# Attention scores as fp16 products over 96 stacked rows per head, in place of fp32 products with block-diagonal keys

## The chip, the cores and the metric

The kernel runs on one NeuronCore of one Trainium2 chip. The metric is the device time of one execution in microseconds (us). TensorE is called PE in the profile, its weight loads PEld, VectorE is DVE, ScalarE is ACT, GpSimd is POOL, and SyncE, which only issues DMA transfers here, is SP. A letter q behind an engine (SPq) marks its instruction queue.

## What is computed

One transformer layer on 4096 tokens of width 512: cross-attention with 16 heads of 32 over a context of 128 positions per batch, and then a feed-forward part with a router, the two best of eight experts, and a shared expert. The change touches only the attention scores.

```python
def _L0_xattn_ref(query, key, value, pad_mask, subsq_mask, Wq, bq, Wk, bk, Wv, bv):
    q = (query @ Wq.T + bq).reshape(n, s, H, d).transpose(0, 2, 1, 3)
    k = (key @ Wk.T + bk).reshape(n, t, H, d).transpose(0, 2, 1, 3)
    v = (value @ Wv.T + bv).reshape(n, t, H, d).transpose(0, 2, 1, 3)
    att = jnp.einsum('bhsd,bhtd->bhst', q, k) / jnp.sqrt(jnp.float32(d))
    att = jnp.where(pad_mask == 0, jnp.float32(-1000000000.0), att)
    att = jnp.where(subsq_mask == 0, jnp.float32(-1000000000.0), att)
    prob = jax.nn.softmax(att, axis=-1)
    out = jnp.einsum('bhst,bhtd->bhsd', prob, v)
...
x = x + jnp.tanh(g_xattn[0]) * _L0_xattn_ref(_layernorm(x, axis=-1), ctx_1024, ctx_1024, ...)
x = x + jnp.tanh(g_ffn[0]) * _L0_ffn_ref(_layernorm(x, axis=-1), ...)
```

## The kernel before

The work is written out by hand for each engine, with semaphores between them. Every engine has one block of code, and inside it the order of the instructions is the order of the source.

Pass 1 handles 32 tiles of 128 tokens: layer norm, queries, attention, second layer norm, router. It is a software pipeline over iterations `it`. In one iteration an engine works on several tiles at once, each at another stage, and a stage with lag L handles tile `it` - L. The helper `pipeline` (L289) writes iterations 0 to 11 out, runs 12 to 31 as a loop of ten pairs (v=0 and v=1), and writes the tail out. Passes 2 (experts, 71 slots) and 3 (shared expert, 32 tiles) follow; they start only when all engines have finished pass 1.

The stages of pass 1 that matter here, by lag:

- Lag 0: SP loads the tile (L377), DVE computes its statistics (L865, L873).
- Lag 2: PE transposes the normed tile into bank 0 (L1038). ACT takes its fp16 high half `x_hi` (L554), DVE the low half `x_lo` (L806). PE computes the queries, transposed, into bank 0 with 48 fp16 matmuls (L1121 to L1123). At the end of its iteration ACT copies them with scale and bias into the fp32 tile `q_t` (four instructions, L605) and raises `q_ready`.
- Lag 3: PE computes the scores of four head groups (`scores(k)`, L1090). Each is one fp32 product of 128 rows and 512 columns: the queries of four heads against `kbd`, which holds the keys of the four heads on the diagonal of 32-row blocks and zeros elsewhere. DVE adds the mask and takes each head's maximum (`maxima(k)`, L776, sixteen instructions a tile). POOL subtracts the maxima (L467), ACT takes exponents (L568, L598).
- Lags 4 to 8: probabilities are transposed and multiplied with the values (L1108), normalised (L788, L790), added to x (L826), normed (L802), routed (L862 and after). SP stores results (L367, L371, L373).

What sets the order around the change: on PE the new tile's transposes (which wait for `q_ready` of the tile before, because bank 0 must be free), two probability transposes, `scores(0)`, `scores(1)`, `mix_values(0)`, `scores(2)`, and so on. DVE's body begins with L802, L806 and `maxima(0)` and ends with `normalise(0, 4)` (L788, L790). Extra work hangs behind the body: the maxima of raw weights in iterations 2 to 10 (L879, 2.27 us each) and a weight split in each second iteration of the loop (L907, 2.35 us). Ahead of tile 0 the keys are computed by PE (L1064), and DVE writes them into `kbd` with sixteen instructions (L757).

## Time and profile before

| what | us |
|---|---|
| median of 3 runs | 1160.58 (1155.75 to 1164.13) |
| the profiled execution, its own time | 1157.58 |
| its span, first to last instruction | 1155.8 |
| pass 1, from the first to the last `maxima` | 44.6 to 491.9 |

The span is the stretch that the trace covers; the execution's own time is 1.8 us more. The times of this document are counted from the span's start. A row's mean duration is that of one instruction and includes the time in the pipeline, so the pace of a row of matmuls is read from their starts. The granted clock is 1.00 when TensorE runs at 2.4 GHz and 0.50 at 1.2 GHz.

### The profile page before, as it was taken

Reading aid. Unit: us, or ns where it says so; the run is one execution under the profiler, and the core shown is the slowest. Engines: PE = TensorE matmul, PEld = TensorE weight load, DVE = VectorE, ACT = ScalarE, POOL = GpSimd, SP = SyncE. Lnnn points to the kernel's source line nnn. Section 1 sums busy time; section 2 is a strip of 40 time slices with the busy share of each in tenths; the row PEclk is TensorE's granted clock in tenths of the full one; section 3 lists DMA queues with packets and bytes.
Section 4 is the critical chain, followed back from the end, with each engine's and each line's share of the span. In section 5 each row is a group of like instructions: output and inputs, shape, how many; then the busy total and the mean of one; then the engine's idle time right before and its main releaser. Section 6 shows DMA issues by size and latency. Waiting matters only on the chain.

```text
span 1155.8 us, 26617 instructions
## 1 busy us (share of the span) xinstructions
PE 1050.2 (91%) x7344; PEld 677.3 (59%) x7345; DVE 822.7 (71%) x2938; ACT 531.4 (46%) x1041; POOL 441.8 (38%) x654
## 2 busy tenths in 40 slices
PE   4699979999999999860899999999999999999997
PEld 3488767777777777660455555555554444444443
DVE  5899868788888888763576666666665666666666
ACT  1366546666666666640444444444443232232322
POOL 3254647676667667442112112112110423232322
PEclk9999889999999999855899999999999999999999
DMA  7555573223323223432233333333332544444543
GB/s 290 197 177 179 131 173 95 93 93 93 93 93 94 94 93 110 101 102 72 74 110 118 115 113 118 118 109 118 118 109 67 185 158 161 157 168 149 169 149 128
DMA packets 76731, 146.96 MB, mean 127 GB/s; under 512 B 20912, under 2 KB 23088, under 8 KB 73872
## 3 DMA queue, kind: packets, MB, share of 16 engines
q1 hardware_dynamic: 46512, 66.01, 20.0%
q10 hardware_dynamic: 17280, 44.83, 10.5%
q0 software_dynamic: 12896, 35.58, 9.9%
q8 instruction: 22, 0.36, 0.2%
q14 instruction: 21, 0.17, 0.1%
HBM read 94.04 MB, written 52.35 MB: 127 GB/s over the span
## 4 chain that ended last, share of the span: by engine, by line
PE 64%; issue 11%; DVE 9%; POOL 8%; ACT 4%; DMA 2%; POOLq 1%; another core or an unknown queue 1%; SPq 0%; DVEq 0%; ACTq 0%
PE bank L1046 15%; PE bank L1047 15%; PE bank L1048 15%; PE bank L1038 8%; PE bank L1090 3%; PE bank L1108 3%; DVE arena L776 3%; POOL arena L467 3%; POOL token_of_row L503 2%; ACT arena L605 1%; DVE arena L865 1%; POOL arena L474 1%; DMA token_of_row<-arena 1%; DVE peak L879 1%; PE bank L1064 1%
## 5 line engine op out<-in xcount | busy, mean ns | idle before, releaser
L1046 PE MATMUL bank<-weights,arena 128*128 (+1 forms) x682 | 259.9, 381 | 2.1 <-ACT arena L647 1.9
L1047 PE MATMUL bank<-weights,arena 128*128 (+1 forms) x682 | 259.8, 381 | 0.0
L1048 PE MATMUL bank<-weights,arena 128*128 (+1 forms) x682 | 259.6, 381 | 0.0
L1038 PE MATMUL bank<-ident,arena 128*128 128x128 f32 (+1 forms) x1592 | 189.4, 267 | 56.1 <-DMA arena<-normed_rows,arena 25.7
L1038 PEld LDWEIGHTS bank<-ident,arena 128*128 128x128 f32 (+1 forms) x1592 | 161.4, 132 | 103.0 <-issue 71.9
L514 POOL DMA_INDIRECT arena<-normed_rows,arena x71 | 67.1, 946 | 254.9 <-PE bank L1038 238.7
L1108 PEld LDWEIGHTS bank<-arena 128*128 128x128 f32 x1024 | 131.7, 198 | 34.3 <-issue 29.5
L1090 PE MATMUL bank<-arena 128*128 128x512 f32 x256 | 138.8, 647 | 5.4 <-DVE arena L776 5.1
L1108 PE MATMUL bank<-arena 128*128 128x33 f32 x1024 | 128.8, 276 | 2.9 <-issue 1.8
L467 POOL TENSOR_TENSOR arena<-arena 128x512 f32<-128x512 f32 x96 | 101.3, 1056 | 76.8 <-DVE arena L776 75.7
L524 POOL DMA_INDIRECT arena<-expert_rows,arena x64 | 62.8, 981 | 173.9 <-DVE arena L998 156.1
L776 DVE CUSTOM_DVE_ANT_0 arena<-bank,arena 128x128 f32<-128x128 f32 x512 | 116.8, 283 | 15.2 <-PE bank L1090 11.1
L568 ACT ACTIVATE arena<-arena 128x512 f32<-128x512 f32 x96 | 60.6, 631 | 119.0 <-POOL arena L467 118.7
L1048 PEld LDWEIGHTS bank<-weights,arena 128*128 128x128 f16 x682 | 67.0, 98 | 80.9 <-issue 1.5
L1046 PEld LDWEIGHTS bank<-weights,arena 128*128 128x128 f16 x682 | 67.1, 98 | 72.1 <-issue 4.4
L1047 PEld LDWEIGHTS bank<-weights,arena 128*128 128x128 f16 x682 | 67.0, 98 | 69.8 <-issue 1.3
L970 DVE TENSOR_SCALAR arena<-bank,arena,w_back 128x512 f32<-128x512 f32 x71 | 57.5, 810 | 55.6 <-PE bank L1048 55.5
L1121 PE MATMUL bank<-arena 128*128 128x128 f16 x512 | 89.2, 221 | 1.4 <-DVE arena L806 1.4
L1122 PE MATMUL bank<-arena 128*128 128x128 f16 x512 | 89.2, 221 | 0.0
L1123 PE MATMUL bank<-arena 128*128 128x128 f16 x512 | 89.1, 221 | 0.0
L503 POOL DMA_INDIRECT token_of_row<-arena x64 | 66.4, 1038 | 39.8 <-POOL arena L500 17.9
L656 ACT ACTIVATE arena<-arena 128x256 f16<-128x256 f32 x71 | 36.0, 508 | 91.3 <-DVE arena L982 91.3
(175 smaller groups left out, 1895.7 us busy)
## 6 DMA issues: line engine op xcount, KB each, us to landing
expert_rows<-arena ACTq DMA_DIRECT2D x71, 256.0 KB, 2.1
arena<-in_x SPq DMA_DIRECT2D x64, 256.0 KB, 3.2
weights<-in_w_gu ACTq DMA_DIRECT2D x8, 1024.0 KB, 4.7
x_rows<-arena SPq DMA_DIRECT2D x32, 256.0 KB
normed_rows<-arena SPq DMA_DIRECT2D x32, 256.0 KB, 4.9
normed_transposed<-arena SPq DMA_DIRECT2D x32, 256.0 KB, 2.3
arena<-normed_transposed SPq DMA_DIRECT2D x32, 256.0 KB, 3.3
arena<-x_rows SPq DMA_DIRECT2D x32, 256.0 KB, 3.4
```

The costliest lines, as they stand in the source:

```text
L467: g.tensor_tensor(sc, sc, mx, ALU.subtract).then_inc(shift_done, 1)
L503: g.indirect_dma_start(list_dram, bass.IndirectOffsetOnAxis(ap=row_i[u][:, k:k + 1], axis=0), tok_i[u], None).then_inc(rows_out[u], 16)
L776: last = d.tensor_tensor_reduce(score[u][:, hh * T:(hh + 1) * T], bank[2 + k % 2][:, h * T:(h + 1) * T], mask_bias[u], 1.0, LOWEST, ALU.ad ...
L1038: last = t.transpose(dst[:, c * P:(c + 1) * P], src[:, c * P:(c + 1) * P], (ident16 if src.dtype == F16 else ident)[:, :])
L1046: t.matmul(dst, hi[:, rows], w_hi(c), start=(c == 0), stop=False)
L1047: t.matmul(dst, hi[:, rows], w_lo(c), start=False, stop=False)
L1048: last = t.matmul(dst, lo[:, rows], w_hi(c), start=False, stop=(c == chunks - 1))
L1090: t.matmul(bank[2 + k % 2][:, :], q_t[u][:, k * P:(k + 1) * P], kbd[:, u, k, :], start=True, stop=True).then_inc(s_done, 1)
L1108: last = t.matmul(bank[6 + half][:, at:at + D + 1], probs_t[k % 2][:, h * P:(h + 1) * P], vaug[:, u, k * HG + h, :], start=True, stop=True)
L1121: t.matmul(dst, wq[:, 0, at:at + P], x_hi[:, xs], start=(ci == 0), stop=False)
L1122: t.matmul(dst, wq[:, 0, at:at + P], x_lo[:, xs], start=False, stop=False)
L1123: last = t.matmul(dst, wq[:, 1, at:at + P], x_hi[:, xs], start=False, stop=(ci == EC - 1))
```

## The change

The scores are computed in fp16 halves. The queries are split: ACT writes the high half of bank 0 into `q_halves` with one instruction, DVE subtracts it and writes the low half, as the last instruction of its body. The product high*high + low*high + high*low is one product over 96 rows when the halves stand under each other: queries as (high, low, high), keys as (high, high, low). For this the rows of four heads, which stand in four blocks of 32 partitions, must be moved into the same 96 partitions. SP does it with twelve DMA transfers for each tile, each of 32 partitions (`stack`). PE then computes each head's scores with one fp16 matmul of 96 rows and 128 columns, sixteen a tile. The bias of the queries goes into the product as a fifth kind of matmul (64 rows, one for each quarter). Scales that keep fp16 in range are undone in the exponent. The keys are treated alike once, after iteration 1: fp32 copy, a maximum over it, a scale found through PE, two halves, twelve transfers. The rest of the diff merges semaphores that counted one by one into ones that count in groups; what they wait for is the same.

```diff
@@ SP, pass 1 body, and the new helper
+                n, j, u = tile(J, v, 2)
+                if live(n, NT):
+                    hold(sp, sp_passed, (q_ready, n + 1))
+                    hold(sp, sp_passed, (s_done, group(n - 2, EC - 1)))
+                    stack(q_stack[u], q_halves, E, (0, 1, 0), q_stacked[u])
+
+            def stack(dst, src, width, parts, done):
+
+                for at, part in enumerate(parts):
+                    for h in range(HG):
+                        sp.dma_start(dst[at * D:(at + 1) * D, h * width:(h + 1) * width],
+                                     src[h * D:(h + 1) * D, part * width:(part + 1) * width]).then_inc(done, 16)
 
             def beside(it):
+                if it == 1:
+                    sp.wait_ge(k_lo_set, 1)
+                    stack(k_stack, k_halves, EC * B * T, (0, 0, 1), k_stacked)
@@ ACT
                     act.wait_ge(q_done, n + 1)
-                    need(act, s_done, group(n - 2, EC - 1))
-                    for c in range(EC):
-                        last = a.activation(q_t[u][:, c * P:(c + 1) * P], bank[0][:, c * P:(c + 1) * P], ACT.Identity,
-                                            scale=w_back[:, 0:1], bias=bq_s[:, c:c + 1])
-                    last.then_inc(q_ready, 1)
+                    hold(act, act_passed, (q_stacked[(v - 3) % 2], 16 * PARTS * (j + u)))
+                    a.activation(q_halves[:, 0:E], bank[0][:, :], ACT.Copy, scale=Q_DOWN).then_inc(q_hi_ready, 1)
 
             def beside(it):
+                if it == 1:
+                    act.wait_ge(scale_set, 3)
+                    a.activation(k_halves[:, 0:EC * B * T], k_full, ACT.Copy, scale=w_scale[:, 5:6]).then_inc(k_hi_set, 1)
@@ DVE, keys_and_values
-                    for h in range(HG):
-                        rows = slice(h * D, (h + 1) * D)
-                        d.tensor_scalar(kbd[rows, :, c, h * T:(h + 1) * T], bank[c][rows, 0:B * T].rearrange("p (b t) -> p b t", b=B),
-                                        bk_s[rows, c:c + 1], float(D) ** -0.5, ALU.add, ALU.mult)
+                    last = d.tensor_scalar(k_full[:, c * B * T:(c + 1) * B * T], bank[c][:, 0:B * T], bk_s[:, c:c + 1],
+                                           float(D) ** -0.5, ALU.add, ALU.mult)
+                link(last)
+                d.tensor_reduce(peak[:, 20:21], k_full, AX.X, ALU.max, apply_absolute_value=True).then_inc(peak_set, 1)
...
+                spread_peaks(7, 2)
+                scale_of(5, 7, 20, SMALL)
...
+                dve.wait_ge(k_hi_set, 1)
+                d.scalar_tensor_tensor(k_halves[:, EC * B * T:], k_full, w_scale[:, 5:6], k_halves[:, 0:EC * B * T],
+                                       ALU.mult, ALU.subtract).then_inc(k_lo_set, 1)
@@ DVE, end of the pass 1 body
                 normalise(0, 4)
+                n, j, u = tile(J, v, 2)
+                if live(n, NT):
+                    dve.wait_ge(q_hi_ready, n + 1)
+                    d.scalar_tensor_tensor(q_halves[:, E:2 * E], bank[0][:, :], Q_DOWN, q_halves[:, 0:E], ALU.mult, ALU.subtract).then_inc(q_ready, 1)
@@ PE
-                        pe.wait_ge(q_ready, n + 1)
+                        pe.wait_ge(q_stacked[u], 16 * PARTS * (j + 1))
+                        pe.wait_ge(k_stacked, 16 * PARTS)
                         need(pe, max_done, group(n, k - 2))
-                        t.matmul(bank[2 + k % 2][:, :], q_t[u][:, k * P:(k + 1) * P], kbd[:, u, k, :],
-                                 start=True, stop=True).then_inc(s_done, 1)
+                        for h in range(HG):
+                            q_at, k_at = (h * EC + k) * P, ((h * EC + k) * B + u) * T
+                            last = t.matmul(bank[2 + k % 2][:, h * T:(h + 1) * T], q_stack[u][0:STACK, q_at:q_at + P],
+                                            k_stack[0:STACK, k_at:k_at + T], start=True, stop=True)
+                        last.then_inc(s_done, 1)
@@ PE, queries
+                            last = t.matmul(dst, bq_half[:, co * P:(co + 1) * P], bias_row[:, :], start=False, stop=True)
```

How the order changes is shown at three places inside the loop. First SP, the second iteration of a pair, before:

```order
L367 DMA x_rows<-arena 128x512
L371 DMA normed_rows<-arena 128x512
L373 ISA
L373 DMA normed_transposed<-arena 128x1024
L377 ISA
L377 DMA arena<-in_x 128x512
L384 ISA
L384 DMA arena<-in_x 128x512
```

and the same iteration in the changed kernel, whose L381 to L398 are the lines L367 to L384 of before, and whose L409 is the new helper:

```order
L381 DMA x_rows<-arena 128x512
L385 DMA normed_rows<-arena 128x512
L387 ISA
L387 DMA normed_transposed<-arena 128x1024
L391 ISA
L391 DMA arena<-in_x 128x512
L398 ISA
L398 DMA arena<-in_x 128x512
L292 ISA
L409 DMA arena<-arena 32x512 x12
```

Twelve transfers stand behind the iteration's last load, and ahead of the next iteration's stores and of its load of x.

Second DVE, between the first and the second iteration of a pair, before (L788 and L790 are `normalise`, L806 is `x_lo`, L776 `maxima(0)`):

```order
L788 RECIPROCAL arena<-bank 128x8
L790 TENSOR_TENSOR arena<-bank,arena 128x256
L802 TENSOR_SCALAR arena<-arena 128x512
L806 SCALAR_TENSOR_TENSOR arena<-bank,arena 128x512
```

and in the changed kernel, with L838 and L840 for `normalise`, L852 for L802 and L856 for L806:

```order
L838 RECIPROCAL arena<-bank 128x8
L840 TENSOR_TENSOR arena<-bank,arena 128x256
L928 SCALAR_TENSOR_TENSOR arena<-bank,arena 128x512
L852 TENSOR_SCALAR arena<-arena 128x512
L856 SCALAR_TENSOR_TENSOR arena<-bank,arena 128x512
```

L928, the low half of the queries, is the body's last instruction, behind everything that the iteration's maxima lead to on DVE.

Third PE, the first part of an iteration, before (L1090 scores, L1108 `mix_values`):

```order
L1038 MATMUL bank<-ident,arena 128x128 x4
L279 ISA
L1090 MATMUL bank<-arena 128x512 x2
L1108 MATMUL bank<-arena 128x33 x4
L279 REGISTER_ALU
L1090 MATMUL bank<-arena 128x512
```

and in the changed kernel (L1142 scores, L1161 `mix_values`):

```order
L1085 MATMUL bank<-ident,arena 128x128 x4
L1137 ISA
L292 ISA
L1142 MATMUL bank<-arena 128x128 x8
L1161 MATMUL bank<-arena 128x33 x4
L292 REGISTER_ALU
L1142 MATMUL bank<-arena 128x128 x4
```

The scores stand where they stood, in four times as many matmuls; everything behind them on PE still stands behind them.

## Rows read from the trace of the kernel before

**Rows 1.** The page: busy time, and the chain that ended last, by engine.

```profile
PE 1050.2 (91%) x7344; PEld 677.3 (59%) x7345; DVE 822.7 (71%) x2938; ACT 531.4 (46%) x1041; POOL 441.8 (38%) x654
...
PE 64%; issue 11%; DVE 9%; POOL 8%; ACT 4%; DMA 2%; POOLq 1%; another core or an unknown queue 1%; SPq 0%; DVEq 0%; ACTq 0%
```

**Rows 2.** Busy us of PE, PEld, DVE, ACT, POOL; granted clock, DMA share, GB/s.

```profile
188.00:484.00 296.00, 276.54 (x2626) 229.57 (x2624) 245.52 (x1307) 196.42 (x426) 195.89 (x275) 0.97 0.34 96
```

**Rows 3.** Waits from 160 to 490 us: total us, times, longest.

```profile
DVE arena L806 <- ACT arena L554: 27.4, 11, 2.8
...
DVE arena L776 <- PE bank L1090: 8.2, 8, 1.8
```

**Rows 4.** Timeline of DVE, one pair of iterations: start, us, line.

```profile
299.26 0.29 DVE L776 CUSTOM_DVE_ANT_0 arena<-bank,arena 128x128 f32<-128x128 f32 x1 [0.76 <-PE bank L1090]
...
308.51 0.42 DVE L790 TENSOR_TENSOR arena<-bank,arena 128x256 f32<-128x256 f32 x1
...
312.66 0.29 DVE L776 CUSTOM_DVE_ANT_0 arena<-bank,arena 128x128 f32<-128x128 f32 x1 [0.35 <-PE bank L1090]
...
321.08 0.69 DVE L862 SCALAR_TENSOR_TENSOR arena<-bank,arena 128x512 f16<-128x512 f32 x1
...
322.86 0.42 DVE L790 TENSOR_TENSOR arena<-bank,arena 128x256 f32<-128x256 f32 x1
```

**Rows 5.** Timeline of DVE: first head of the maxima of tile 0 and of tile 31.

```profile
44.62 0.28 DVE L776 CUSTOM_DVE_ANT_0 arena<-bank,arena 128x128 f32<-128x128 f32 x1
...
485.58 0.28 DVE L776 CUSTOM_DVE_ANT_0 arena<-bank,arena 128x128 f32<-128x128 f32 x1
```

**Rows 6.** Timeline of SP's queue: DMA issues that follow one another.

```profile
83.40 0.33 SPq L380 DMA_DIRECT2D arena<-in_sub  x1
83.78 0.43 SPq L384 DMA_DIRECT2D arena<-in_x  x1
84.25 0.43 SPq L367 DMA_DIRECT2D x_rows<-arena  x1
...
321.94 0.33 SPq L373 DMA_DIRECT2D normed_transposed<-arena  x1
322.46 0.35 SPq L377 DMA_DIRECT2D arena<-in_x  x1
323.01 0.35 SPq L384 DMA_DIRECT2D arena<-in_x  x1
```

**Rows 7.** The page: DMA issues, KB each, median us from issue to landing.

```profile
expert_rows<-arena ACTq DMA_DIRECT2D x71, 256.0 KB, 2.1
arena<-in_x SPq DMA_DIRECT2D x64, 256.0 KB, 3.2
...
arena<-token_of_row SPq DMA_DIRECT2D x71, 0.5 KB, 2.0
```

**Rows 8.** Timeline of PE: four records of scores, and two third matmuls of the queries.

```profile
311.25 1.88 PE L1090 MATMUL bank<-arena 128*128 128x512 f32 x4
...
317.89 0.22 PE L1123 MATMUL bank<-arena 128*128 128x128 f16 x1
...
318.06 0.22 PE L1123 MATMUL bank<-arena 128*128 128x128 f16 x1
```

**Rows 9.** Two stretches, columns as in rows 2.

```profile
322.00:324.00 2.00, 0.72 (x18) 0.62 (x17) 1.70 (x7) 2.00 (x8) 0.81 (x3) 1.00 0.72 245
324.00:327.00 3.00, 2.74 (x13) 2.77 (x14) 0.48 (x1) 2.98 (x4) 1.85 (x4) 0.50 0.46 167
```

**Rows 10.** The page: SP's DMA queue: packets, MB, share of 16 engines.

```profile
q1 hardware_dynamic: 46512, 66.01, 20.0%
```

**Rows 11.** Timeline of DVE: a scale found through PE, and the keys.

```profile
14.54 0.29 DVE L719 TENSOR_REDUCE peak_top<-bank 128x1 f32<-128x128 f32 x1 [0.63 <-PE bank L1054]
...
16.69 0.14 DVE L739 TENSOR_SCALAR w_scale<-w_scale 128x1 f32<-128x1 f32 x1
...
25.19 7.91 DVE L757 TENSOR_SCALAR arena<-bank,bk_s 32x256 f32<-32x256 f32 x16 [1.86 <-PE bank L1064]
```

175 lines of the change are left out of this document (102 added, 73 removed).

## The prediction

> **What bounds the kernel now.** I began with the page. PE is busy for 91% of the span and carries 64% of the chain that ended last [rows 1], which suggests that cheaper scores would pay in full. But that is a mean over three passes, and the change lies in pass 1 alone. There the first head's maximum of tile 0 starts at 44.62 and that of tile 31 at 485.58 [rows 5]: 31 iterations in 441.0 us, 14.23 us each. The windows of the steady part show two engines near their limit: of 296 us PE is busy for 276.5 and DVE for 245.5 [rows 2], that is 93% and 83%. DVE's largest waits from 160 to 490 us are 27.4 us for `x_hi` from ACT and 8.2 us for scores from PE [rows 3], together 1.8 us an iteration over 20 to 23 iterations. So PE's work is no long way ahead of DVE's: DVE has 245.5 * 14.23 / 296 = 11.8 us of work in each 14.23 us.
>
> The timeline then gives the shape of an iteration on DVE. From the first maximum to the end of the body it takes from 299.26 to 308.51 + 0.4 = 9.65 us in one iteration and from 312.66 to 322.86 + 0.4 = 10.6 us in the next [rows 4], nearly all of it work. This stretch is the number on which the forecast rests.
>
> **The change, PE.** Four scores were eight records in pairs. Four records take 1.88 us, so a tile's scores take 3.8 us [rows 8]. Queries show the pace of fp16 matmuls with 128 columns: three in 318.06 - 317.89 = 0.17 us, 0.057 each [rows 8]. Sixteen for the scores and four for the bias are 1.1 us. PE is relieved of 2.7 us an iteration.
>
> **ACT and DVE.** ACT issues one instruction in place of four and comes out ahead. DVE gets one more, from bank 0 to fp16 with 512 columns; L862 is the same form and takes 0.69 us [rows 4]. The small scale added to `peaks_neg` and to the exponents costs nothing, since the instructions are the same.
>
> **The transfers, and the ring they close.** Before, the queries left PE in the middle of the iteration, ACT copied them, and they were there when PE reached `scores(0)`; DVE had no part in it. Now the low half is DVE's last instruction of the body, SP waits for it, issues twelve transfers, and PE may start `scores(0)` of the next iteration only when the twelfth has landed. DVE's `maxima(0)` waits for that score, and the body behind `maxima(0)` ends again in the low half. So the time of an iteration is the sum of this ring, and nothing in it can start early:
>
> - DVE from `maxima(0)` to the end of the body: 9.65 and 10.6 us. I take 10.0, because the 10.6 holds some collisions with POOL's row scatter that will fall into the new wait.
> - The low half: 0.7.
> - SP wakes: L862 ends at 321.77 and L373 is issued at 321.94, 0.2 [rows 4, 6].
> - Eleven issue intervals until the twelfth is issued. Pairs that follow one another stand 0.38, 0.47 and at most 0.55 us apart [rows 6]. No transfer of 32 partitions is in the trace; those there have 128. I take 0.45, near the back-to-back row, and get 4.95. Both ends are kept: 4.2 and 6.05.
> - Issue to landing of the last: 2.0 for 0.5 KB, 2.1 to 3.2 for 256 KB [rows 7]. A copy is 32 KB and stays in SBUF, so I take 2.0.
> - Four matmuls, their way through PE and the signal to DVE: 0.5, from 0.22 us for one and the 0.2 to 0.35 that DVE sits until PE's score [rows 4, 8].
>
> The sum is 10.0 + 0.7 + 0.2 + 4.95 + 2.0 + 0.5 = 18.35 us, against 14.23: 4.1 us more in each of 31 iterations, 128 us. What was beside is now hidden in the 7.6 us in which DVE waits: L907, the peaks of the weights, and also `x_lo`, since bank 0 is free when the wait begins. PE's 2.7 us fall into the same hole, so the gain is worth nothing. The bytes are no limit: 12 * 32 packets of 1 KB at the queue's mean (20% of 16 * 1155.8 us over 46512 packets [rows 10], 0.08 us) are 384 * 0.08 / 16 = 1.9 us on each engine, less than the issues take.
>
> Queued behind the waits: on SP the stores and the load of x of the next iteration, now issued some 7 us after DVE's body ends, and landed 3.2 us later [rows 7], about 10.5 after it; DVE needs them 7.6 + 7.5 later, so nobody waits. On PE `mix_values` and the rest stand behind `scores(0)`; DVE reaches what depends on them only 3 us or more after its first maximum. ACT's new wait, for the transfers of the tile before, is over when PE has begun that tile's scores.
>
> The Trainium skill (DMA: Bandwidth & Descriptors, "Rules for kernel authors") says that many small transfers should be merged, that below 64 KB one pays mostly overhead, and that transfers to disjoint parts of the partitions gain nothing over one of 128. That speaks against this change: by this rule the twelve copies cost like twelve full ones, and the sum would go with the 0.47 of the rows, 130 us in place of 128.
>
> **The start.** `kbd` took 16 instructions of 0.48 us [rows 11]. Four replace them, but then come a maximum of 1024 columns (1.2 us by L879's 2.27 for 2048), a scale through PE (from 14.54 to 16.83, 2.3 us [rows 11]), the high half on ACT and the low half on DVE (1.1 to 1.2 each, half of L907's 2.35), and twelve transfers (5.4 us). The load of x for tile 2 stands behind these on SP; DVE needs it in iteration 2 ahead of the low half. By these terms: keys on DVE to 33.3 as now, scale 35.7, halves 38.1, copies issued 43.7, x landed 46.9, low half 48.5, first maximum 56.2 in place of 44.6. I take 12 us.
>
> **Sum.** 1157.6 + 128 + 12 = 1298 us on the profiled execution; the median of the runs shown lies 3 us above it, so I say 1300. Passes 2 and 3 are unchanged.
>
> **Rivals.**
>
> 1. The copies are cheap to issue (fewer partitions, fewer descriptors): 0.1 us each. The ring is 10.0 + 0.7 + 0.2 + 1.1 + 2.0 + 0.5 = 14.5, 0.3 more than now. With the start at 3 to 8 us the time is about 1168, at 0.05 us each 1155. For it: the row of smallest busy time, 0.33, may be the price of 128 partitions. Against: 64 KB (L380) and 256 KB (L373) both show 0.33 [rows 6], so size does not set it. Chance 0.07.
> 2. PE is the bound, and the copies do not show, because landing is short as well. PE's 2.7 us are then gained until DVE stops it: 11.8 + 0.7 = 12.5 of work, 1.7 less than 14.23, 54 us: 1104. For it: PE's 93% [rows 2]. Against: it needs the ring below 12.5, hence less than 1.1 us for twelve copies with their landing, and 2.0 is the shortest landing shown. Chance 0.06.
> 3. TensorE's clock. After a stretch in which PE was busy for 0.72 of 2 us the granted clock went from 1.00 to 0.50 [rows 9], from 2.4 to 1.2 GHz. Each iteration will now have a hole of 7 us. If the whole iteration then runs at 1.2 GHz, PE's way from `scores(0)` to the last query, which was 311.25 to 320.5 (48 matmuls of 0.057 from 317.8 on [rows 8]) and without 2.7 us is 6.6, doubles to 13.1; with 0.7 on ACT the low half starts 13.8 after the scores in place of 10.3. The ring is 13.8 + 0.7 + 0.2 + 4.95 + 2.0 = 21.7, 7.4 over now: 1157.6 + 229 + 12, about 1400. Against: the mean clock over the steady part is 0.97 [rows 2], so such lapses were short, and after a short one the low half is hardly late, because PE's way has 3 us of room. Chance 0.08.
>
> The Trainium skill (TensorE: Matmul & The Clock Gate, "HAM oscillation") describes a loop whose wait for a DMA drops the clock in every turn. Rival 3 is the strong form of it; the mild form lies in my range.
>
> **How the numbers follow.** The forecast has 0.79. Its own range: low 9.65 + 0.7 + 0.2 + 4.2 + 2.0 + 0.3 = 17.0, which with 8 us at the start is 1252, and as a 32-partition copy may be cheaper than any shown I go to 1225; high 10.6 + 0.7 + 0.2 + 6.05 + 3.3 + 0.5 = 21.35, with 12 us 1390. To leave out no more than 2 in 10 the range takes in rival 3: 1225 to 1425. Below it lie rivals 1 and 2. Differences of less than 1% can hardly be told from none. Slower: 0.79 + 0.08 = 0.87. Same: 0.07, faster: 0.06.
>
> **What would show it.** Right: SP's issues of L409 in rows of twelve, about 5 us long; PE's `scores(0)` waiting for a DMA, 31 times, 5 us or more; DVE idle ahead of the first L826 of each tile; iterations of 18 us. Wrong: issues below 0.2 us apart; DVE's L928 waiting for ACT by more than a microsecond (then PE or ACT sets the ring); or PE without idle time in pass 1.

## The result, and the profile after

The changed kernel takes 1467.5 us (median of 4 runs, 1464.1 to 1469.7); the kernel before took 1161.2 us in the same comparison. The ratio is 1.264, with a 95% interval from 1.259 to 1.270. The forecast was 1300 us with a range up to 1425: the direction was right, the size was less than half of the truth, and the time lies outside the range.

The page of the changed kernel, first the busy times, PE's busy share and granted clock in 40 equal slices (in tenths), then the chain that ended last, by engine and by line (compare [rows 1]), and two groups of instructions with their busy time, the mean ns of one, and the idle time before them:

```profile
span 1462.3 us, 28278 instructions
...
PE 1117.0 (76%) x7731; PEld 780.3 (53%) x7732; DVE 833.7 (57%) x2970; ACT 530.9 (36%) x946; POOL 439.6 (30%) x658
...
PE   4366754857575766767657259999999999999997
...
PEclk9567676667676767777676569999999999999999
...
PE 67%; SPq 15%; DMA 8%; DVE 3%; issue 3%; ACT 2%; POOLq 1%; POOL 0%; ACTq 0%; DVEq 0%
SPq L409 15%; PE bank L1093 12%; PE bank L1094 12%; PE bank L1095 12%; PE bank L1085 10%; PE bank L1161 7%; DMA arena<-arena 6%; PE bank L1142 4%; PE bank L1174 3%; PE bank L1175 2%; PE bank L1176 2%; DVE arena L928 2%; PE bank L1177 1%; ACT arena L641 1%; DMA token_of_row<-arena 1%
...
L1142 PE MATMUL bank<-arena 96*128 96x128 f16 x512 | 72.3, 308 | 254.5 <-DMA arena<-arena 253.6
...
L826 DVE CUSTOM_DVE_ANT_0 arena<-bank,arena 128x128 f32<-128x128 f32 x512 | 116.8, 283 | 243.9 <-PE bank L1142 240.5
```

In the chain, SP's queue goes from 0% to 15%, all of it issues of the copies (L409), and DMA from 2% to 8%, of which 6% is the landing of copies. PE stood idle for 253.6 us ahead of the scores until a transfer landed, and DVE for 240.5 us until the scores came. The windows, with columns as in [rows 2], put this in pass 1:

```profile
319.00:765.00 446.00, 294.63 (x2622) 274.49 (x2622) 232.77 (x1224) 179.29 (x333) 176.17 (x254) 0.72 0.24 74
825.00:1462.00 637.00, 595.30 (x3257) 301.60 (x3257) 400.94 (x847) 227.05 (x382) 143.96 (x204) 0.97 0.40 126
```

From 319 to 765 us PE is 66% busy (93% in [rows 2]), DVE 52% (83%), and the mean granted clock is 0.72 (0.97). The last stretch, with passes 2 and 3, is back at 0.97.

One iteration of the ring, on DVE, SP's queue, PE and ACT (start us, us, line; in brackets the idle time ahead and who ended it):

```profile
435.79 0.69 DVE L928 SCALAR_TENSOR_TENSOR arena<-bank,arena 128x512 f16<-128x512 f32 x1 [2.57 <-ACT arena L641]
...
448.34 0.29 DVE L826 CUSTOM_DVE_ANT_0 arena<-bank,arena 128x128 f32<-128x128 f32 x1 [9.29 <-PE bank L1142]
...
457.62 0.42 DVE L840 TENSOR_TENSOR arena<-bank,arena 128x256 f32<-128x256 f32 x1
460.34 0.69 DVE L928 SCALAR_TENSOR_TENSOR arena<-bank,arena 128x512 f16<-128x512 f32 x1 [2.29 <-ACT arena L641]
```

```profile
436.73 7.50 SPq L409 DMA_DIRECT2D arena<-arena  x12
444.43 0.43 SPq L381 DMA_DIRECT2D x_rows<-arena  x1
```

```profile
447.46 1.03 PE L1142 MATMUL bank<-arena 96*128 96x128 f16 x8 [8.89 <-DMA arena<-arena]
...
452.44 2.76 PE L1085 MATMUL bank<-ident,arena 128*128 128x128 f32 x12
...
459.28 0.23 PE L1177 MATMUL bank<-bias_row,bq_half 64*128 64x128 f16 x1
```

```profile
459.71 0.60 ACT L641 ACTIVATE arena<-bank 128x512 f16<-128x512 f32 x1 [1.72 <-PE bank L1177]
```

The low half starts at 435.79, twelve issues run from 436.73 to 436.73 + 7.50 = 444.23, PE starts the scores at 447.46, DVE its first maximum at 448.34, and the body ends at 457.62 + 0.42 = 458.04. DVE then waits 2.3 us for ACT's high half, which waits for PE's last bias product. The whole is 24.55 us.

The same readings were made of all 31 intervals from one low half to the next, and of every experiment. In the tables below, "issues" run from the start of the first copy's issue to the end of the last one's; "landing" is from the start of the last issue to PE's first score (one issue taken as 0.59); "answer" goes from there to DVE's first maximum, "body" to DVE's end of body, "wait" to the next low half. The issues less 0.59, the other terms and the 0.86 of the low half and SP's wake add up to the iteration. The means, in us:

| term | forecast | changed kernel |
|---|---|---|
| low half and SP's wake | 0.9 | 0.86 |
| start of the first issue to start of the twelfth | 4.95 | 7.62 - 0.59 = 7.03 |
| landing of the twelfth | 2.0 | 2.97 |
| answer | 0.5 | 0.84 |
| body | 10.0 | 9.46 |
| wait of the low half for ACT | 0 | 2.19 |
| sum | 18.35 | 23.35 |

On the span the account closes. DVE's first maximum of tile 0 and that of tile 31 (compare [rows 5]):

```profile
54.12 0.69 DVE L915 BATCH_NORM_STATS2 arena<-arena 128x6 f32<-128x512 f32 x1 [15.72 <-DMA arena<-in_x]
...
65.04 0.29 DVE L826 CUSTOM_DVE_ANT_0 arena<-bank,arena 128x128 f32<-128x128 f32 x1 [4.45 <-PE bank L1142]
...
790.06 0.29 DVE L826 CUSTOM_DVE_ANT_0 arena<-bank,arena 128x128 f32<-128x128 f32 x1 [6.67 <-PE bank L1142]
```

The 31 iterations take 725.0 us in place of 441.0, which is 284.0 more. The first maximum comes 20.4 us later (65.04 for 44.62). Together 304.4, of 306.5 us between the spans; 2 us are left for the rest.

### The profile page after: what moved, and what is told of

Read it like the earlier page. It is cut to its first block, busy times and chain, and to the rows that moved or that the text cites. A ratio compares the mean times of both kernels' runs of the same rounds, so it can differ in the third digit from the quotient of the medians.

```text
span 1462.3 us, 28278 instructions
## 1 busy us (share of the span) xinstructions
PE 1117.0 (76%) x7731; PEld 780.3 (53%) x7732; DVE 833.7 (57%) x2970; ACT 530.9 (36%) x946; POOL 439.6 (30%) x658
## 4 chain that ended last, share of the span: by engine, by line
PE 67%; SPq 15%; DMA 8%; DVE 3%; issue 3%; ACT 2%; POOLq 1%; POOL 0%; ACTq 0%; DVEq 0%
SPq L409 15%; PE bank L1093 12%; PE bank L1094 12%; PE bank L1095 12%; PE bank L1085 10%; PE bank L1161 7%; DMA arena<-arena 6%; PE bank L1142 4%; PE bank L1174 3%; PE bank L1175 2%; PE bank L1176 2%; DVE arena L928 2%; PE bank L1177 1%; ACT arena L641 1%; DMA token_of_row<-arena 1%
## 5 line engine op out<-in xcount | busy, mean ns | idle before, releaser
L1142 PE MATMUL bank<-arena 96*128 96x128 f16 x512 | 72.3, 308 | 254.5 <-DMA arena<-arena 253.6
L1085 PE MATMUL bank<-ident,arena 128*128 128x128 f32 (+1 forms) x1592 | 220.3, 294 | 49.0 <-DMA arena<-normed_rows,arena 28.5
L826 DVE CUSTOM_DVE_ANT_0 arena<-bank,arena 128x128 f32<-128x128 f32 x512 | 116.8, 283 | 243.9 <-PE bank L1142 240.5
L1085 PEld LDWEIGHTS bank<-ident,arena 128*128 128x128 f32 (+1 forms) x1592 | 189.5, 149 | 75.4 <-issue 44.4
L504 POOL TENSOR_TENSOR arena<-arena 128x512 f32<-128x512 f32 x96 | 106.4, 1109 | 362.9 <-DVE arena L826 362.0
L1142 PEld LDWEIGHTS bank<-arena 96*128 96x128 f16 x512 | 59.9, 159 | 263.0 <-issue 157.9
L605 ACT ACTIVATE arena<-arena,score_scale 128x512 f32<-128x512 f32 x96 | 68.9, 717 | 340.7 <-POOL arena L504 340.7
L1161 PE MATMUL bank<-arena 128*128 128x33 f32 x1024 | 182.3, 338 | 1.8 <-ACT arena L598 1.8
L1161 PEld LDWEIGHTS bank<-arena 128*128 128x128 f32 x1024 | 177.0, 263 | 4.0 <-ACT arena L598 2.0
L1174 PE MATMUL bank<-arena 128*128 128x128 f16 x512 | 109.7, 243 | 2.2 <-DVE arena L856 2.2
L1175 PE MATMUL bank<-arena 128*128 128x128 f16 x512 | 108.5, 241 | 0.0
L1176 PE MATMUL bank<-arena 128*128 128x128 f16 x512 | 107.7, 240 | 0.0
L540 POOL DMA_INDIRECT token_of_row<-arena x64 | 77.8, 1215 | 39.2 <-POOL arena L537 18.5
```

What stands on the lines that cost most here:

```text
L504: g.tensor_tensor(sc, sc, mx, ALU.subtract).then_inc(shift_done, 1)
L826: last = d.tensor_tensor_reduce(score[u][:, hh * T:(hh + 1) * T], bank[2 + k % 2][:, h * T:(h + 1) * T], mask_bias[u], 1.0, LOWEST, ALU.ad ...
L1085: last = t.transpose(dst[:, c * P:(c + 1) * P], src[:, c * P:(c + 1) * P], (ident16 if src.dtype == F16 else ident)[:, :])
L1142: last = t.matmul(bank[2 + k % 2][:, h * T:(h + 1) * T], q_stack[u][0:STACK, q_at:q_at + P], k_stack[0:STACK, k_at:k_at + T], start=True, ...
L1161: last = t.matmul(bank[6 + half][:, at:at + D + 1], probs_t[k % 2][:, h * P:(h + 1) * P], vaug[:, u, k * HG + h, :], start=True, stop=True)
L1174: t.matmul(dst, wq[:, 0, at:at + P], x_hi[:, xs], start=(ci == 0), stop=False)
```

## The experiments

Theory A was the prediction's, with the sizes mended: the ring sets the iteration, and the number of issues is its largest added term. Rivals were the low granted clock of TensorE (B in the first runs, C in e5_bd16, K in f3_warm60), the bytes of the copies (C in the first runs), VectorE's low half (B in e5_bd16), and, after the first runs, other traffic that stretches the landing (D). The ratios are to the kernel before, timed again in each group of runs: 1155.9 us for e1 to e4, 1165.3 for e5, e6, e7 and e9, 1165.2 for f1 to f3, 1168.1 for g1 and g2. So a difference of 1% in us between runs of different groups is not to be read alone; the terms of the iteration, read from the traces, stand beside it.

### Keep TensorE busy while it waits: e1_warm, f3_warm60

```diff
+                n3, j3, u3 = tile(J, v, 3)
+                if live(n3, NT):
+                    for _ in range(120):
+                        t.matmul(bank[7][:, 384:512], ones[:, :], before[:, :], start=True, stop=True)
                 scores(0)
```

f3_warm60 has `range(60)`.

> The changed kernel with 120 fp16 matmuls of 128 columns, whose result nobody reads, in PE's order just ahead of the wait of scores(0), so that TensorE works while the copies travel. Theory A (the ring of DVE body, low half, twelve issues, landing and scores sets the iteration, and the clock is one term of it): the granted clock stays near 1.00 in pass 1, L928 no longer waits some 2 us for ACT, the scores answer 0.4 us sooner, so 31 * 2.4 = 75 us go, about 1392. Theory B (the clock makes up all of the 5 us by which the iteration of 23.3 us is longer than the 18.35 forecast): 31 * 5 = 153 us go, about 1315. Theory C (the bytes of the copies and of the stores behind them hold the DMA engines): no change, 1467.

Measured: 1455.8 us, ratio 1.258 (1.247 to 1.269). That lies between the expectations, and the interval takes in the changed kernel's 1.264: of the 75 us that theory A gave to the clock, next to nothing came.

> The changed kernel (1467) with 60 idle fp16 products of 128 columns of TensorE ahead of its wait for the copies (e1_warm had 120, which ended after the copies had landed in part of the iterations: scores started 0.9 to 1.2 us later). Theory K (the 2.1 us that the low half waits for ScalarE, and 0.4 us of the answer, are TensorE at half clock after its idle stretch): 60 products end by themselves before the copies land, the wait falls to 0.7 or less and the answer to 0.6, -1.7 x31 = -53: about 1415. Rival (that wait has another cause, or the clock falls again before the query products): 1450 to 1467.

Measured: 1486.6 us, ratio 1.277 (1.271 to 1.284), about 1% slower than the changed kernel (1467.5) and above both expectations.

| | issues | landing | answer | wait | iteration | clock, 319 to 765 us |
|---|---|---|---|---|---|---|
| changed kernel | 7.62 | 2.97 | 0.84 | 2.19 | 23.35 | 0.72 |
| e1_warm | 8.04 | 3.47 | 0.66 | 1.40 | 23.15 | 0.87 |
| f3_warm60 | 7.92 | 3.30 | 0.79 | 2.16 | 23.89 | 0.79 |

With 120 products the wait falls by 0.79 and the answer by 0.18, while scores start 0.92 later, so little is left. With 60 products neither falls by more than 0.05. The windows of one iteration of f3_warm60 show why: the scores and transposes, then the queries, then the idle products (452 to 455.2), then PE's idle stretch.

```profile
439.70:441.60 1.90, 1.90 (x13) 1.90 (x13) 1.65 (x9) 1.76 (x4) 1.63 (x4) 0.50 0.00 0
441.60:444.20 2.60, 2.60 (x15) 2.54 (x13) 2.60 (x21) 1.53 (x3) 2.45 (x3) 0.50 0.47 126
444.20:450.00 5.80, 5.80 (x73) 5.11 (x72) 4.29 (x21) 4.53 (x9) 2.48 (x7) 0.97 0.00 0
450.00:452.00 2.00, 2.00 (x34) 1.99 (x33) 0.57 (x2) 1.92 (x4) 1.53 (x2) 1.00 0.13 33
452.00:455.20 3.20, 3.13 (x57) 2.95 (x53) 0.26 (x1) 0.54 (x2) 0.00 (x0) 1.00 0.20 52
455.20:462.00 6.80, 0.00 (x0) 0.00 (x0) 0.00 (x0) 0.00 (x0) 0.00 (x0) 0.72 0.68 129
```

The 60 products ran at a granted clock of 1.00, that is 2.4 GHz, and were done in 3.5 us. PE was idle for 6.8 us behind them, the granted clock fell in that stretch (mean 0.72), and the scores of the next iteration, from 462.06, ran at 0.50 (1.2 GHz) again, like those in the first two rows. So my expectation of 1415 fell for a reason of its own design: the filler stood at the wrong end of the hole. The mean over a whole iteration hides this. From the first score to the last bias product the mean granted clock is 0.63 in the changed kernel, 0.64 in f3_warm60 and 0.76 in e1_warm, and the waits are 2.19, 2.16 and 1.40 us: the wait moves with the clock of that stretch. Why issues and landing are 0.3 to 0.5 us longer each in both runs is open, and a filler that spans the hole exactly was not tried.

### Half the issues on ACT's queue: e2_split

```diff
-                    stack(q_stack[u], q_halves, E, (0, 1, 0), q_stacked[u])
+                    stack(q_stack[u], q_halves, E, (0, 1, 0), q_stacked[u], range(0, HG, 2))
...
+                        for h in range(1, HG, 2):
+                            act.dma_start(q_stack[u][at * D:(at + 1) * D, h * E:(h + 1) * E],
+                                          q_halves[h * D:(h + 1) * D, part * E:(part + 1) * E]).then_inc(q_stacked[u], 16)
```

> The changed kernel with half of the query copies (heads 1 and 3 of each block, six of twelve) issued by ACT behind its high half, and six by SP. Theory A (each queue pays 0.63 us for each issue by itself): six intervals of 0.63 go, 3.8 us in each of 31 iterations, about 1350. Theory A2 (the pace of 0.63 is that of something that both queues share): no change, 1467. Theory C (bytes): no change either, but then the landing of the last copy grows by what the issues save.

Measured: 1421.4 us, ratio 1.228 (1.218 to 1.239), 71 us above theory A's 1350. SP's six issues take 3.94 us in place of 7.62, as theory A had it, so 3.68 are won. But the landing grows from 2.97 to 9.69 - 0.86 - 3.94 + 0.59 = 5.48 us, and only 1.10 us an iteration are left (22.25). ACT's last issue starts 0.1 us ahead of SP's last on the mean, so it isn't that. The trace has what it is: in the first six iterations, ahead of POOL's first token scatter, the landing is 2.25 us on the mean, and in the other 25 it is 6.26, and PE's first score comes 1.5 us after the last scatter has landed (the two times go together over these 25 with a correlation of 0.97). The Trainium skill ("Perfetto Trace Analysis", section "DMA Optimizations") says that if descriptor generation is the bottleneck, balancing DMAs across the engines that can issue them may help. This case agrees for the issues, and shows that most of it was given back at the landing.

### A third of the copies: e3_four

```diff
-                    stack(q_stack[u], q_halves, E, (0, 1, 0), q_stacked[u])
+                    stack(q_stack[u], q_halves, E, (0,), q_stacked[u])
...
-                            last = t.matmul(bank[2 + k % 2][:, h * T:(h + 1) * T], q_stack[u][0:STACK, q_at:q_at + P],
-                                            k_stack[0:STACK, k_at:k_at + T], start=True, stop=True)
+                            last = t.matmul(bank[2 + k % 2][:, h * T:(h + 1) * T], q_stack[u][0:D, q_at:q_at + P],
+                                            k_stack[0:D, k_at:k_at + T], start=True, stop=True)
```

The products with a low half are left out.

> The changed kernel with four of the twelve query copies (only the high half, once) and scores over 32 rows in place of 96; the low-half products are left out. Theory A: eight issue intervals of 0.63 us go, 5.0 us an iteration, 156 us, and a shorter hole lets the clock recover sooner, for up to 2 us more: 1250 to 1310. Theory B (clock alone): the hole is still 4 us long and the clock still falls, so at most 60 us go, 1405. Theory C (bytes): two thirds of the landing time beyond 2.0 us go, about 1 us an iteration, 1435.

Measured: 1408.3 us, ratio 1.217 (1.207 to 1.227). Four issues take 2.53 us, 5.09 fewer, and yet the iteration is only 1.61 us shorter (21.74), because the landing is 5.57 us in place of 2.97. It missed theory A's 1250 to 1310 by 100 us. Something in these 5.57 us was not the copies' own; this started theory D.

### Fewer bytes, same number: e9_thin

```diff
-                        sp.dma_start(dst[at * D:(at + 1) * D, h * width:(h + 1) * width],
-                                     src[h * D:(h + 1) * D, part * width:(part + 1) * width]).then_inc(done, 16)
+                        cols = 64 if width == E else width
+                        sp.dma_start(dst[at * D:(at + 1) * D, h * width:h * width + cols],
+                                     src[h * D:(h + 1) * D, part * width:part * width + cols]).then_inc(done, 16)
```

> The changed kernel (1467) with each of the twelve query copies cut from 512 columns to 64 (the rest of the stacked queries stays zero, so most of the product is left out): the number of issues is the same, the bytes are an eighth. Theory A (the issue of twelve copies is the cost): issues stay 0.6 apart, 7.5 us together, the time stays within 1430 to 1470. Bytes (the data of the copies take the time): issue phase falls to the 0.45 of other transfers and the landing to 2, -(1.8+0.8) x31 = -80, about 1385 or less.

Measured: 1479.5 us, ratio 1.270 (1.262 to 1.278). That is 10 us above theory A's range, and by the ratio not to be told from the changed kernel (1.264). Its queue shows the same row as with 32 KB:

```profile
445.68 7.50 SPq L411 DMA_DIRECT2D arena<-arena  x12
```

An eighth of the bytes saves nothing. The bytes of the copies are out as a cause, both at the issue and at the landing (3.32 us, with 2.97 before).

### Wider copies: g2_wide

```diff
-                    stack(q_stack[u], q_halves, E, (0,), q_stacked[u])
+                    for at, part in enumerate((0, 1, 0, 1)):
+                        sp.dma_start(q_stack[u][:, at * E:(at + 1) * E], q_halves[:, part * E:(part + 1) * E]).then_inc(q_stacked[u], 16)
```

> The kernel e3_four (four copies, products with the low halves left out: 1408) with each of its four copies over 128 partitions of 512 columns in place of 32 (four times the bytes; the heads are then not stacked, so the scores are of other numbers). Theory N (an issue costs by the instruction, whatever it carries): 0.6 apart as before and about 1408 to 1430. Rival W (32 partitions of one transfer are what makes issue or landing slow): issues 0.45 apart, landing 2 to 3 us shorter, 1320 to 1380.

Measured: 1429.9 us, ratio 1.224 (1.210 to 1.239), against 1408.3 and 1.217 for e3_four with four copies of 32 partitions; the intervals overlap (the landing is 6.08 us, 0.5 more). The issues, and those of SP's other transfers behind them:

```profile
461.45 2.41 SPq L404 DMA_DIRECT2D arena<-arena  x4
464.06 0.43 SPq L381 DMA_DIRECT2D x_rows<-arena  x1
...
465.18 0.33 SPq L387 DMA_DIRECT2D normed_transposed<-arena  x1
```

Four wide copies of 128 KB take 2.41 us, four narrow ones 2.53: an issue of such a copy is about 0.6 us whatever it carries, which is theory N. Transfers of 128 partitions to or from HBM on the same queue are 0.33 to 0.43 each here; in the changed kernel that is the range of their medians, and single ones take 0.58 and more. So width and bytes don't explain the difference. What the copies have and the others lack is that both ends are in on-chip memory; that this is the cause was not tried alone.

### What stretches the landing: e6_stores_wait, e7_scatter_late, g1_late_full

e6_stores_wait is e3_four with SP waiting for the copies before its stores:

```diff
                     stack(q_stack[u], q_halves, E, (0,), q_stacked[u])
+                    hold(sp, sp_passed, (q_stacked[u], 16 * HG * (j + 1)))
```

> The kernel e3_four (four copies, products with the low halves left out: 1408) with one addition: SP waits until the copies have landed before it issues the stores and the load behind them. D2 (transfers issued behind the copies on the same queues stretch their landing): the last copy lands some 2 us after its issue instead of 5.5, -3.5 x31 = -110, about 1300. D1 (the token scatters of POOL stretch it) or neither: no change, 1408, up to 1430 as SP's stores and loads come later.

Measured: 1396.5 us, ratio 1.199 (1.191 to 1.206). The landing goes from 5.57 to 5.23 us, and the iteration is 0.38 us shorter, 12 us in all, of the 110 that D2 asked for: D2 falls as the main cause.

e7_scatter_late is e3_four with POOL's token scatters (L540) one iteration later, behind the shift:

```diff
-        LAG1, LAG2, LAG3, SPAN2 = 8, 4, 4, 4
+        LAG1, LAG2, LAG3, SPAN2 = 9, 4, 4, 4
...
                 shift(2)
+                n, j, u = tile(J, v, 9)
+                if live(n, NT):
+                    need(pool, rows_out[u], 16 * TOP * j)
...
+                    for k in range(TOP):
+                        g.indirect_dma_start(list_dram, bass.IndirectOffsetOnAxis(ap=row_i[u][:, k:k + 1], axis=0),
...
-                n, j, u = tile(J, v, 8)
-                if live(n, NT):
-                    need(pool, rows_out[u], 16 * TOP * j)
...
-                    for k in range(TOP):
-                        g.indirect_dma_start(list_dram, bass.IndirectOffsetOnAxis(ap=row_i[u][:, k:k + 1], axis=0),
```

> The kernel e3_four (four copies, products with the low halves left out: 1408) with one change: POOL's two token scatters of an iteration are issued one iteration later, behind the shift. D1 (these scatters, issued just ahead of the copies, stretch their landing): landing 5.5 to 2 us, -3.5 x31 = -110, about 1300 and up to 1310 with the longer tail. D2 (SP's stores and load behind the copies stretch it): no change, 1408 to 1420.

Measured: 1324.4 us, ratio 1.137 (1.130 to 1.144), 84 us less than e3_four: D1 holds, though 110 us were expected. The landing is 3.21 us instead of 5.57, and the iteration 18.95 instead of 21.74. First POOL in e3_four, with its scatters:

```profile
454.63 1.09 POOL L540 DMA_INDIRECT token_of_row<-arena  x1 [0.86 <-POOL arena L537]
456.03 0.96 POOL L540 DMA_INDIRECT token_of_row<-arena  x1 [0.30 <-issue]
```

Then the chain of e3_four in the same iteration (start us, us, what):

```profile
456.35 0.52 SPq L409
456.92 0.58 SPq L409
457.56 0.58 SPq L409
458.18 5.50 DMA arena<-arena
463.80 1.03 PE bank L1142 x8
```

And that of e7_scatter_late, in which the last scatter is issued 3.9 us ahead of the first copy (first its row on POOL, then the chain):

```profile
448.53 0.98 POOL L526 DMA_INDIRECT token_of_row<-arena  x1 [0.30 <-issue]
...
452.46 0.52 SPq L409
453.03 0.59 SPq L409
453.67 0.58 SPq L409
454.29 1.88 DMA arena<-arena
456.30 0.61 PE bank L1142 x8
```

From the start of its issue to its landing, the last of the same four copies takes 5.50 us behind two scatters of POOL, a different queue, and 1.88 with the scatters moved away. The Trainium skill ("DMA: Bandwidth & Descriptors", section "Queues, rings and completion order") says that a transfer's semaphore write is strongly ordered and lands only after every earlier write of its DMA engine, across the queues. The 1.5 us between the scatters' landing and the scores in e2_split agree with it, but no run here looks at the order itself, and in 7 of 25 iterations of e3_four the copies landed ahead of the second scatter.

g1_late_full does the same with all twelve copies in place.

> The changed kernel (1467) with POOL's two token scatters issued one iteration later, as in e7_scatter_late, but with all twelve copies kept. With four copies that took 2.6 us from the landing of an iteration (1408 to 1324). Theory D1a (the scatters delay whatever copies are in flight): the last of the twelve lands up to 2 us earlier too: about 1400 to 1430. D1b (the scatters are over by the time that the last of twelve is issued, 7.5 us after the first, so their price was already hidden in the issues): 1455 to 1475.

Measured: 1444.0 us, ratio 1.236 (1.231 to 1.242), 23.5 us less than the changed kernel. The landing is 10.13 - 0.86 - 7.65 + 0.59 = 2.21 us instead of 2.97, the iteration 22.69. This lies between D1a and D1b: with 7.6 us of issues ahead of the last copy, most of the scatters' price is hidden, and 0.8 us of it is not. In 30 of the 31 iterations the landing is now 1.9 to 2.0 us. In the other it is 10.2: there ACT's queue had issued three loads of weights (1 MB each) at 230.72, just ahead of the copies at 232.06.

### The copies off the ring: e4_lag

One more iteration lies between the queries and the scores, and SP issues the copies behind its load of x:

```diff
-        LAG1, LAG2, LAG3, SPAN2 = 8, 4, 4, 4
+        LAG1, LAG2, LAG3, SPAN2 = 9, 4, 4, 4
...
+                n, j, u = tile(J, v, 3)
+                if live(n, NT):
+                    hold(sp, sp_passed, (q_ready, n + 1))
```

> The changed kernel with one more iteration between the queries and the scores: all stages behind the queries move from lag k to k + 1, the copies are issued by SP at the start of the iteration after the queries, behind the load of x, and PE needs them only in the iteration after that. Copies, bytes, matmuls and instructions are the same. Theory A (the ring is the cost): the ring is cut, the copies have 13 us to land, and the iteration falls to the work of DVE, 12.5 to 13.5 us, so that pass 1 is 20 to 50 us shorter than before, plus one iteration in the tail and 14 us at the start: 1130 to 1170. Theory B (clock): PE still has 25% idle time, the iteration stays over 16 us: above 1220. Theory C (bytes or SP's own time, 12 * 0.63 + 6 * 0.5 = 10.6 us an iteration): it stays above 15 us, 1190 or more.

Measured: 1210.2 us, ratio 1.045 (1.038 to 1.052). The iteration falls to 14.97 us, although the twelve issues still take 7.5 in most of them and the landing is as long as 8.25 in one. The first row is of the chain that ended last, the second of ACT:

```profile
324.13 8.25 DMA arena<-arena
...
332.49 0.60 ACT L644 ACTIVATE arena<-bank 128x512 f16<-128x512 f32 x1 [1.31 <-DMA arena<-arena]
```

PE no longer waits for copies in pass 1, but a looser ring is left: ACT's next high half goes into the buffer that the copies read, and must wait for them. It did so six times, 12.7 us in all. The iteration is still no longer than that of the next kernel, which has no copies (15.29), so theory C (bytes, or SP's own time) falls as well, though 1210 lies in its range. The place of the copies in the ring cost (23.35 - 14.97) * 31 = 260 us; as work beside it they cost little. My 1130 to 1170 was still too good: the low half and a start that is 28.7 us later (first maximum at 73.33) stay.

### No copies at all: e5_bd16, f2_nolow

The keys stand block-diagonally in fp16 halves (ACT and DVE write them there once, in four parts each), and the scores are three products over the queries as they are:

```diff
-                            last = t.matmul(bank[2 + k % 2][:, h * T:(h + 1) * T], q_stack[u][0:STACK, q_at:q_at + P],
-                                            k_stack[0:STACK, k_at:k_at + T], start=True, stop=True)
+                        t.matmul(dst, hi, kbd[:, 0, u, k, :], start=True, stop=False)
+                        t.matmul(dst, hi, kbd[:, 1, u, k, :], start=False, stop=False)
+                        last = t.matmul(dst, lo, kbd[:, 0, u, k, :], start=False, stop=True)
```

> This kernel has no stacking copies: the keys stand block-diagonally in fp16 halves and the scores are three fp16 products of 512 columns over the unstacked halves (high x high, high x low, low x high), so the same sum reaches the scores. Theory D and theory A (the loss is the twelve copies, by their landing or by their issue) both: the ring becomes maxima to body end 9.5 + wait and low half 2.9 + three products and answer 1.5 = about 13.9 a iteration, 23.35 - 13.9 = 9.4 saved, x31 = 290: about 1175, range 1130 to 1200. Rival C (the cold clock of pass 1 is what costs, and products on fp16 don't warm it): over 1250. Rival B (the added DVE low half and the ACT wait before it cost most): over 1220.

Measured: 1202.7 us, ratio 1.034 (1.029 to 1.040), 2.7 us above the expected range. The first maxima are at 58.30 and 532.22 us, so the iterations take 15.29 us and the start costs 13.7. In the window of [rows 2]:

```profile
188.00:484.00 296.00, 273.79 (x2623) 226.20 (x2621) 243.21 (x1274) 178.90 (x343) 188.15 (x262) 0.93 0.35 91
```

PE is 92% busy again with a clock of 0.93, and the low half waits for ACT 0.67 us, no longer 2.19. Rivals C and B, which asked for over 1250 and over 1220, fall.

f2_nolow takes from this kernel the low half of the queries and the two products with a low half.

> The kernel e5_bd16 (1203) without the low half of the queries and without the two products that carry a low half; the scores are the product of the high halves alone, so that part is left out. Theory S: the low half's 0.69 us and the wait ahead of it leave VectorE's order and two products of 0.21 us leave the ring, about 1.1 x31 = 34: about 1169. Rival R (the low half is hidden beside other work): 1195 to 1205.

Measured: 1162.8 us, ratio 0.999 (0.995 to 1.002). The iterations take (494.06 - 55.92) / 31 = 14.13 us: the low half, its wait and two products were 1.16 us each time, 36 us. The late start (55.92 for 44.62) is left. Theory S holds.

### The scores undone, the rest kept: f1_fp32

```diff
-                        t.matmul(dst, hi, kbd[:, 0, u, k, :], start=True, stop=False)
-                        t.matmul(dst, hi, kbd[:, 1, u, k, :], start=False, stop=False)
-                        last = t.matmul(dst, lo, kbd[:, 0, u, k, :], start=False, stop=True)
+                        last = t.matmul(bank[2 + k % 2][:, :], q_t[u][:, k * P:(k + 1) * P], kbd[:, u, k, :], start=True, stop=True)
```

(against e5_bd16; `q_t` is one 128x512 pass of ACT, `kbd` is fp32 again, and the bias stays a product.)

> The scores of before (four fp32 products with block-diagonal keys, no halves, no copies) with the rest of the change kept: the query bias as a product of TensorE, one 128x512 pass of ScalarE in place of four with bias, the merged semaphores, the scale of the scores inside Exp. Theory S (what is left of e5_bd16's +40 is the low half on VectorE and the split of the keys): no low half and no split, about 1155 to 1170, the same as before. Rival R (the rest of the change, bias product and late first scores, costs it): about 1195 to 1205, as e5_bd16. Rival G (one pass in place of four frees ScalarE and the ring): under 1150, faster than before.

Measured: 1160.5 us over 10 runs, ratio 0.997 (0.995 to 0.9995).

```profile
188.00:484.00 296.00, 292.24 (x2716) 235.57 (x2714) 242.26 (x1313) 191.41 (x363) 193.95 (x275) 0.98 0.38 96
```

PE is at 99% here, against the 93% of [rows 2], and the iterations take (483.43 - 44.78) / 31 = 14.15 us against 14.23. Rivals R and G fall, and S holds: everything that the change loses is in the way the scores are made. The bias product and the single pass are worth 0.3%, at the edge of what can be measured. Among the versions that leave nothing out it is the only one at or below the kernel before.

## Why the prediction was wrong

- **The ring** was right. SP's issues, the landing, the scores and DVE's body stand one behind the other in every iteration, and e4_lag shows the place: with the same copies outside it, 260 us are gone. What the prediction said of PE, that its work falls into the hole, did not hold, because PE's way ends last (below).
- **Issue intervals, 0.45 forecast: wrong.** The step took rows of transfers to and from HBM [rows 6] for copies within the chip. They are 7.03 / 11 = 0.64 us apart; e9_thin and g2_wide show that neither bytes nor width set this. The bound of 0.55 that I kept was too low as well. +2.08 us, 64 us in all. This is the first of the two terms that failed most. (The 130 us that the prediction gives for intervals of 0.47 should read 135: 0.02 * 11 * 31 is 7 us more than 128.)
- **The low half's wait for ACT, 0 forecast: wrong.** I had a row for this (rival 3) and gave it a chance of 0.08 as an all-or-nothing case. The wait is 2.19 us, 68 us in all. In the changed kernel the granted clock is 0.50 from 444 to 455 us, while the scores, the values and the transposes run, and comes up only for the queries; ahead of it stands a stretch in which PE did nothing:

```profile
440.00:444.00 4.00, 0.00 (x0) 0.00 (x0) 0.00 (x0) 0.00 (x0) 0.00 (x0) 0.88 0.19 50
444.00:446.50 2.50, 0.00 (x0) 0.00 (x0) 0.00 (x0) 0.00 (x0) 0.00 (x0) 0.50 0.57 198
446.50:449.00 2.50, 1.54 (x12) 1.55 (x12) 0.66 (x7) 0.00 (x0) 0.00 (x0) 0.50 1.04 313
449.00:452.00 3.00, 3.00 (x18) 3.00 (x18) 2.59 (x19) 1.56 (x4) 2.56 (x4) 0.50 0.09 33
452.00:455.00 3.00, 3.00 (x18) 2.94 (x18) 3.00 (x22) 2.01 (x4) 1.83 (x2) 0.50 0.00 0
455.00:458.00 3.00, 3.00 (x35) 2.51 (x34) 2.95 (x19) 2.75 (x6) 1.04 (x4) 0.72 0.00 0
```

  The lapse was not short: it covers the first 7.5 us of PE's way (447.46 to 455), and that way, not DVE's body, ends last. How much of the wait is the clock can be read from PE's way itself, from the first score to the end of the last bias product. Two iterations of the changed kernel, then one of e4_lag, with the same matmuls in the same order:

```profile
422.31:434.96 12.65, 12.65 (x97) 11.69 (x97) 9.35 (x61) 6.20 (x13) 7.07 (x12) 0.59 0.19 51
698.71:709.86 11.15, 11.15 (x97) 10.46 (x97) 9.35 (x61) 6.13 (x13) 6.46 (x10) 0.68 0.38 123
275.65:284.29 8.64, 8.18 (x99) 7.22 (x96) 8.11 (x56) 6.50 (x14) 5.31 (x8) 1.00 0.32 99
```

  The low half then waits 2.57 us in the first (row at 435.79) and 1.07 in the second. It can start 0.83 us after PE's way ends (459.51 and 460.34 in the iteration above), and the body ends 0.84 + 9.46 = 10.3 us after the first score. At a clock of 1.00 that is 8.64 + 0.83 = 9.5, ahead of the body's end; so by this estimate the 2.19 is the clock, and next to nothing would be left without the lapse. (The longest such stretch of e4_lag's later iterations at 1.00 is 9.65, with PE idle for 1.3 us of it, which would leave 0.2.) It also shows that the room was 0.8 us and not the 3 of the prediction: PE's way at full clock is 8.64 us, not 6.6. A part of that is the four bias products, put at 0.06 us each; in e4_lag each holds the queries up by 0.25. The three mechanisms (issues, landing, clock) add up; I had made the clock a rival to the forecast, with DVE's L928 waiting for ACT as its sign, and it was a part of it.
- **Landing, 2.0 forecast, 2.97 measured.** +0.97 us, 30 us. The 2.0 and 2.1 of [rows 7] are medians of transfers elsewhere. Here POOL's token scatters are in flight, and with few copies that shows in full (5.57 us). Moving them gives 0.76 of the 0.97 back (g1_late_full), and the rest is the one iteration with the loads of weights ahead of the copies. The prediction had set no row for traffic of other queues beside the copies.
- **Answer, 0.5 forecast, 0.84 measured,** +0.34 us or 11 us; 0.66 in e1_warm, so about half of it is the clock.
- **Body, 10.0 forecast, 9.46 measured,** -17 us. That is less than either iteration of [rows 4] had, as the prediction argued from the collisions with POOL's scatter; no run tries them alone.
- **The start, 12 forecast, 20.4 measured.** The copies of the keys began at 37.8 us, as forecast (38.1), but the twelve took 8.96 us instead of 5.4. The load of x behind them then landed 7.3 us after its issue instead of 3.2: DVE waited 15.72 us for it in the row at 54.12. The low half came at 55.0 in place of 48.5, and the first ring took 10.1 in place of 7.7 (the prediction's own terms make that 8.35).
- **The sum**: (2.08 + 2.19 + 0.97 + 0.34 - 0.54 - 0.04) * 31 = 155, and 8 at the start, make 163 of the 167 us that were missing.
- **Rivals 1 and 2** (cheap issues, PE as the bound) fell at once. What the prediction took from the Trainium skill ("DMA: Bandwidth & Descriptors", section "Rules for kernel authors") on many small transfers was borne out in kind: four copies of 32 partitions took 2.53 us to issue and four of 128 took 2.41. Only the price of a full one was that of another route.

## What to carry to other kernels

Before a transfer is put between two engines of a software pipeline, follow the cycle that it closes: here twelve copies inside it cost 260 us more than outside it. Take the price of an issue from a transfer of the same route, count the transfers and not the bytes, and look for what other queues have in flight when it should land. And where each turn leaves TensorE idle for several microseconds (8.9 here), look at what the granted clock does behind the hole (0.50 for 7.5 us here), and price its work there as a term of the sum and not as a rival to it.

## What the runs showed of the hardware that was not expected

- The issue of a copy within on-chip memory takes 0.59 us on SP's queue, with 4, 32 or 128 KB and with 32 or 128 partitions, against medians of 0.33 to 0.43 for transfers of 256 KB to or from HBM on the same queue.
- Two indirect scatters of POOL, issued just ahead of the copies or beside their first, move the landing of four copies from 3.21 to 5.57 us on the mean.
- When the issues were shared between two queues (e2_split), their span was halved and the landing rose from 2.97 to 5.48 us. The rise is in the 25 iterations with scatters (6.26 us, and 2.25 in the six ahead of the first). So POOL's scatters are its likely cause, as in e7_scatter_late, but the split with the scatters moved was not tried.
